# One query buffer per unit with the shift written into it, and one block of values per key step

## The chip, the cores and the metric

The program runs on one core of a Trainium2 chip. The metric is the device time of one execution in microseconds (us), as a median of several runs; smaller is better. The engines are named as the profile names them: PE (TensorE matmuls), PEld (its weight loads), DVE (VectorE), ACT (ScalarE), POOL (GpSimd) and SP (SyncE, which issues DMAs).

## The reference

Two transformer layers on a sequence of S = 2048 rows of D = 128 values. Layer 0: x += attention(norm(x)), causal, 16 heads of 8 values, rotary embedding; then x += a gated network with 512 hidden values and two more 512 x 512 layers. Layer 1: x += attention(norm(x)) over all keys, 16 heads of 8, with low-rank projections and biases; then x += a mixture of 8 experts (top 2). The attention of both layers is, for each head:

```python
scores = einsum('bhsd,bhtd->bhst', q, k) / scale
attn = softmax(scores)          # layer 0: only keys t <= s
out = einsum('bhst,bhtd->bhsd', attn, v)
```

## The kernel before

The program is a row of phases, each a block in which all engines run their own instruction lists, tied by semaphores. The change lies in `attention_phase` (L306), which runs once per layer.

**Units and steps.** The queries are cut into C = 4 column blocks of CW = 512, the heads into G = 4 groups of four. A unit is a column block c with a group g, 16 units per layer in the order of `units`. A unit goes through its keys in steps of 128: 16 steps in layer 1, 4(c + 1) in layer 0, where the last four steps of a unit lie on the diagonal and use only columns from `first_col` on (512, 384, 256, 128 of them). A step has four scores (one per head, j = 0 to 3, below S0 to S3): 64 rows of K against 64 rows of queries, written to a PSUM bank of 512 columns (L442). Heads 0 and 2 lie in rows 0 to 63 of the array, heads 1 and 3 in rows 64 to 127. ACT takes exp of each bank into `probs` (L536), and PE multiplies `probs` with V (`values`, L455), accumulating in the bank `acc`; each head uses 9 columns of its own strip of 32 of the array. A value matmul is float32 and counts as two instructions.

**Precision by split rows.** A block of K or Q holds two heads, each in 64 partitions: products of high and low halves of the numbers in the first 32, and extra rows from `SHIFT_ROW` = 32 on. In these K has ones, and the query buffer the negated maximum of the row (high and low part), so that the score comes out already shifted. There are two query buffers: `Qm` without the shift, used for the maxima, and `Qx` with it, used for the scores.

**Maxima.** For a unit the maximum of each query's scores is wanted before the unit starts. `score_maxima` (L423) makes scores the other way round (queries as weights, 512 keys streaming), two heads into a pair of PSUM banks, and DVE reduces the pair (L556). There are two pairs; the next but one use of a pair waits for its reduction (`m_done`). `plan(n)` spreads the reductions of units n + 1 and n + 2 over the 2 x steps slots of unit n. In layer 1 that is one per slot, in layer 0 it depends on the units' sizes. The last two units have fewer or none. Then DVE forms the negated maxima and writes them to `shiftM` (L576, L580).

**Banks and jobs.** Three PSUM banks (`E_BANKS`) are used in turn by all jobs that ACT evacuates: scores, and query builds. Job e waits until job e - 3 is evacuated:

```python
def wait_bank(e):
    if e >= E_BANKS:
        pe.wait_ge(e_done, e - E_BANKS + 1)
```

PE takes jobs, maxima and values in the order of `unit(n)` (L471): per step, for b = 0 and 1, two scores, then after the first step `build_qm(n + 2)` and after the last but one `build_qx(n + 1)`, then the slot's maxima, then half of the values of the step before (`values_part`, L460; in step 0 of a unit that is the last step of the unit before, and the values of a step 0 and those narrower than 256 columns are one block at b = 1). `build_qm` has for each of two blocks two matmuls (L393, L394), which ACT copies into `Qm` (L515). `build_qx` has the same and four more 128-column matmuls with `shiftM` (L407), and ACT copies into `Qx`. Before the first unit of a layer PE makes the maxima of units 0 and 1 and `build_qx(0)`. In layer 0, POOL masks the diagonal blocks of `probs` (L508) before the values may use them. ACT does the exponentials of step k only when the values of step k - 2 are done (`pv_done`). DVE copies `acc` out once per unit (L584).

## Time and profile before

| | |
|---|---|
| median of 3 runs | 1938.62 us (1923.58 to 1941.95) |
| the profiled execution | 1926.7 us |
| its span, first to last instruction | 1924.8 us |
| mean granted clock of TensorE over the span | 0.892 |
| PE / DVE / ACT / POOL busy | 1793.8 / 1157.7 / 1130.8 / 82.1 us |

Times in the profile are of the one profiled execution, from the first instruction on. A granted clock of 1 is 2.4 GHz, of 0.5 is 1.2 GHz. "PE busy" counts the time in which at least one matmul record is open. A record opens when the matmul's turn has come, so a matmul that waits for its own weight load is counted from then. Matmuls in different halves of the array run side by side, and a merged row of the timeline shows how many (x2, x8) lie in it.

### The profile page before, as it was taken

The numbers are of one execution on the slowest core, as the hardware profiler recorded it, in microseconds if no ns is written. First come the engines' busy times: TensorE is split into PE (matmuls) and PEld (weight loads), VectorE is DVE, ScalarE is ACT, GpSimd is POOL, SyncE is SP. The second block draws the span as 40 slices with busy tenths as digits, with TensorE's granted clock in tenths as the row PEclk, the third lists the DMA queues.
The fourth block names the chain that finished last, engine by engine and source line by source line (L and its number), as shares of the span: only waits on it lengthen the run. The fifth ranks groups of instructions, "written<-read, shape, count | busy, mean of one in ns | idle before, by whom it ended". The sixth has DMA issues, their size and how long they took to land. (4 is left out here: it accounts for less than half of the span.)

```text
span 1924.8 us, 31645 instructions
## 1 busy us (share of the span) xinstructions
PE 1793.8 (93%) x13000; PEld 830.1 (43%) x13000; DVE 1157.7 (60%) x1566; ACT 1130.8 (59%) x2092; POOL 82.1 (4%) x158
## 2 busy tenths in 40 slices
PE   6999999999998999677999999999999999689999
PEld 3544434444334444332333333333333333457676
DVE  7556686777614100469788988988898860611111
ACT  3436566667774322230788878878887887233433
POOL 3011101000000000020000000000000000000000
PEclk9558898888888999775899999999999999789999
DMA  2100000000000000100000000000000000010000
GB/s 98 61 1 2 1 1 1 1 1 1 1 1 1 1 0 0 51 1 0 1 1 1 2 1 1 1 2 1 1 2 1 1 1 1 1 34 11 22 22 22
DMA packets 16766, 17.12 MB, mean 9 GB/s; under 512 B 2994, under 2 KB 13695, under 8 KB 16127
## 3 DMA queue, kind: packets, MB, share of 16 engines
q1 hardware_dynamic: 16639, 15.32, 2.5%
q8 instruction: 93, 1.52, 0.3%
q14 instruction: 34, 0.28, 0.0%
HBM read 14.26 MB, written 1.05 MB: 8 GB/s over the span
## 5 line engine op out<-in xcount | busy, mean ns | idle before, releaser
L556 DVE TENSOR_REDUCE maxp<-banks 128x2 f32<-128x1024 f32 (+3 forms) x800 | 942.7, 1200 | 253.2 <-PE banks L423 145.0
L536 ACT ACTIVATE probs<-banks 128x512 f32<-128x512 f32 (+3 forms) x1664 | 855.7, 571 | 274.8 <-PE banks L442 255.8
L455 PE MATMUL banks<-probs,V 128*9 128x256 f32 (+3 forms) x6272 | 516.0, 403 | 6.9 <-POOL probs L508 6.2
L442 PE MATMUL banks<-Qx,K 64*128 64x512 f32 (+3 forms) x1664 | 460.6, 512 | 6.6 <-ACT probs L536 6.3
L423 PE MATMUL banks<-K,Qm 64*128 64x512 f32 (+3 forms) x1664 | 389.5, 452 | 30.7 <-DVE maxp L556 30.0
L442 PEld LDWEIGHTS banks<-Qx,K 64*128 64x128 f32 x1664 | 188.9, 197 | 390.8 <-ACT probs L536 316.6
L423 PEld LDWEIGHTS banks<-K,Qm 64*128 64x128 f32 x1664 | 187.6, 211 | 83.3 <-DVE maxp L556 67.6
L455 PEld LDWEIGHTS banks<-probs,V 128*9 128x9 f32 x6272 | 93.7, 89 | 261.7 <-ACT probs L536 192.3
L945 DVE SCALAR_TENSOR_TENSOR x<-banks,wts,x 128x128 f32<-128x128 f32 x128 | 36.0, 344 | 195.9 <-PE banks L908 195.9
L933 ACT ACTIVATE work<-banks,eb 128x512 f32<-128x512 f32 x128 | 86.4, 688 | 104.3 <-PE banks L899 101.9
L908 PEld LDWEIGHTS banks<-work 128*128 128x128 f32 x1024 | 118.1, 192 | 11.5 <-issue 11.5
L899 PE MATMUL banks<-xnT,work 128*128 128x512 f32 x256 | 116.0, 601 | 5.0 <-DMA eb<-in_eb 5.0
L908 PE MATMUL banks<-work 128*128 128x128 f32 x1024 | 118.2, 275 | 0.0
L733 PE MATMUL banks<-work,flex 128*128 128x512 f32 x256 | 110.5, 592 | 0.0
L515 ACT ACTIVATE Qx<-banks 128x512 fp32r<-128x512 f32 x64 | 38.2, 597 | 103.6 <-PE banks L407 103.6
L584 DVE COPY outT<-banks 128x512 f32<-128x512 f32 x32 | 21.9, 683 | 97.2 <-PE banks L455 97.2
L771 DVE TENSOR_TENSOR work<-banks,s_rows 128x128 f32<-128x128 f32 x16 | 3.5, 284 | 122.4 <-PE banks L740 122.4
L733 PEld LDWEIGHTS banks<-work,flex 128*128 128x128 f32 x256 | 48.6, 190 | 61.2 <-issue 61.2
L393 PE MATMUL banks<-qb,sel 32*128 32x512 f32 x128 | 69.0, 551 | 6.2 <-PEq L145 3.3
L508 POOL TENSOR_SCALAR_AFFINE_SELECT probs<-probs 128x256 f32<-128x256 f32 x128 | 52.3, 408 | 503.4 <-ACT probs L536 502.8
L899 PEld LDWEIGHTS banks<-xnT,work 128*128 128x128 f32 x256 | 47.6, 194 | 56.3 <-issue 53.1
L756 ACT ACTIVATE work<-banks,sh 128x512 f32<-128x512 f32 x32 | 22.0, 687 | 82.7 <-PE banks L733 82.7
(126 smaller groups left out, 921.6 us busy)
## 6 DMA issues: line engine op xcount, KB each, us to landing
tables<-in_tables SPq DMA_DIRECT2D x2, 2048.0 KB, 9.6
work<-in_ew SPq DMA_DIRECT2D x16, 256.0 KB, 2.9
flex<-in_h SPq DMA_DIRECT2D x2, 1024.0 KB, 7.8
x<-in_x SPq DMA_DIRECT2D x4, 256.0 KB, 4.1
out<-x SPq DMA_DIRECT2D x4, 256.0 KB, 2.3
cst<-in_consts SPq DMA_DIRECT2D x1, 864.5 KB, 5.8
flex<-in_w SPq DMA_DIRECT2D x3, 256.0 KB, 3.0
flex<-in_w_qk SPq DMA_DIRECT2D x1, 256.0 KB, 5.9
```

The lines of the kernel that those rows point to most:

```text
L393: pe.matmul(ebank(e), k.sel[rows, SEL_QHI, b, :], k.qb[rows, 0, c * CW:(c + 1) * CW], start=True, stop=False)
L423: mm = pe.matmul(out, k.Qm[rows, n % 2, b, t * P:(t + 1) * P], k.K[rows, 2 * g + b, a * CW:a * CW + w], start=True, stop=True)
L442: mm = pe.matmul(ebank(e)[:, first:CW], k.K[rows, 2 * g + b, kt * P:(kt + 1) * P], k.Qx[rows, n % 2, b, first:CW], start=True, stop=True)
L455: mm = pe.matmul(acc[32 * j:32 * j + HD + 1, low:high], k.V9[:, kt, g * HG + j, :], k.probs[:, slot + j, low:high], start=(kt == 0), stop= ...
L508: pool.affine_select(out=tile, in_=tile, compare_op=ALU.is_ge, fill=0.0, base=0, pattern=[[0, 2], [1, P]], channel_multiplier=-1).then_inc ...
L515: act.activation(dst, ebank(e), ACT.Copy).then_inc(e_done, 1)
L536: act.activation(k.probs[:, HG * (s % 2) + j, first:CW], ebank(e)[:, first:CW], ACT.Exp, scale=scale).then_inc(e_done, 1)
L556: dve.tensor_reduce(dst, src, AX.X, ALU.max).then_inc(m_done, 1)
L733: mm = pe.matmul(hb[m % 2][:, :], w[:, b, m * P:(m + 1) * P], src[:, b, :], start=(b == 0), stop=(b == HB - 1))
L899: pe.matmul(ub[m][:, :], k.ew1[:, q, m * P:(m + 1) * P], k.xnT[:, c * CW:(c + 1) * CW], start=True, stop=True).then_inc(up_ready, 1)
L908: mm = pe.matmul(yb[c % 2][:, t * P:(t + 1) * P], k.hid[:, c % 2, b, t * P:(t + 1) * P], k.ew2[:, q, b, :], start=(b == 0), stop=(b == HB ...
L933: act.activation(k.hid[:, c % 2, m, :], ub[m][:, :], ACT.Gelu, bias=k.eb1[:, q, m:m + 1]).then_inc(act_ready, 1)
```

## The change

What it does: the two query buffers of a unit become one, `Q`, three deep. `build_queries` writes it without the shift (as `build_qm` did); the maxima read it; later `turn_shift` turns the negated maxima by four 128-column matmuls into one bank, and ACT writes them with two copies (32 partitions, both blocks at once, 2 x 512 columns each) into the rows of `Q` from SHIFT_ROW on. The two blocks of a buffer have shift rows of their own, so the ones of K lie in two rows or the other by the block's parity. In a step, PE now does S0, S1, the first slot's maxima, S2, the second slot's maxima with the upper half of the array first, S3, and then all columns of the values of the step before in one block. In step 0 and in the last but one, S3 comes before the build or the turned shift, and the second slot's maxima after it. The jobs keep their three banks and are numbered from a list.

```diff
@@ -260,7 +260,7 @@
                     low_half(i - 1)
             for r in range(len(rounds)):
                 dve.wait_ge(k_psum, r + 1)
-                dve.tensor_scalar(built(r, 0), k.banks[:, 4 * (r % 2):4 * (r % 2) + 2, :], k.ones_col[:, 0:1], None, ALU.add
+                dve.tensor_scalar(built(r, 0), k.banks[:, 4 * (r % 2):4 * (r % 2) + 2, :], k.ones_col[:, rounds[r][1]:rounds[r][1] + 1], None, ALU.add
                                   ).then_inc(k_built_dve, 1)
 
         @block.gpsimd
...
@@ -326,19 +326,22 @@
     m_base = [sum(len(reductions(m)) for m in range(n)) for n in range(NU + 1)]
     s_base = [sum(steps[:n]) for n in range(NU + 1)]
 
-    e_base = [6]
-    for n in range(NU):
-        e_base.append(e_base[n] + HG * steps[n] + 2 * (n + 2 < NU) + 2 * (n + 1 < NU))
-    qx_after = [steps[n] - 2 for n in range(NU)]
-
-    def qm_job(n, b):
-        return 2 * n + b if n < 2 else e_base[n - 2] + HG + b
-
-    def qx_job(n, b):
-        return 4 + b if n == 0 else e_base[n - 1] + HG * (qx_after[n - 1] + 1) + 2 * (n + 1 < NU) + b
-
-    def exp_job(n, kt, j):
-        return e_base[n] + HG * kt + j + 2 * (kt > 0 and n + 2 < NU) + 2 * (kt > qx_after[n] and n + 1 < NU)
+    shift_after = [steps[n] - 2 for n in range(NU)]
+
+    def exp_bank_jobs():
+        for n in (0, 1):
+            yield from (("queries", n, b) for b in (0, 1))
+        yield ("shift", 0)
+        for n in range(NU):
+            for kt in range(steps[n]):
+                yield from (("scores", n, kt, j) for j in range(HG))
+                if kt == 0 and n + 2 < NU:
+                    yield from (("queries", n + 2, b) for b in (0, 1))
+                if kt == shift_after[n] and n + 1 < NU:
+                    yield ("shift", n + 1)
+
+    e_number = {job: number for number, job in enumerate(exp_bank_jobs())}
+    exp_job = lambda n, kt, j: e_number["scores", n, kt, j]
 
     masks = {n: TC * units[n][0] for n in range(NU)} if causal else {}
     mask_base = lambda n, kt: 2 * (TC * n + kt - masks[n])
...
@@ -386,41 +389,38 @@
                 if e >= E_BANKS:
                     pe.wait_ge(e_done, e - E_BANKS + 1)
 
-            def plain_queries(n, b, e):
+            def build_queries(n):
                 c, g = units[n]
                 rows = slice(32 * g, 32 * g + 32)
+                for b in (0, 1):
+                    e = e_number["queries", n, b]
+                    wait_bank(e)
+                    pe.matmul(ebank(e), k.sel[rows, SEL_QHI, b, :], k.qb[rows, 0, c * CW:(c + 1) * CW],
+                              start=True, stop=False)
+                    pe.matmul(ebank(e), k.sel[rows, SEL_QLO, b, :], k.qb[rows, 1, c * CW:(c + 1) * CW],
+                              start=False, stop=True).then_inc(e_ready, 1)
+
+            def turn_shift(n):
+                e = e_number["shift", n]
                 wait_bank(e)
-                pe.matmul(ebank(e), k.sel[rows, SEL_QHI, b, :], k.qb[rows, 0, c * CW:(c + 1) * CW], start=True, stop=False)
-                return pe.matmul(ebank(e), k.sel[rows, SEL_QLO, b, :], k.qb[rows, 1, c * CW:(c + 1) * CW],
-                                 start=False, stop=True)
-
-            def build_qm(n):
-                for b in (0, 1):
-                    plain_queries(n, b, qm_job(n, b)).then_inc(e_ready, 1)
-
-            def build_qx(n):
                 pe.wait_ge(shift_ready, n + 1)
-                for b in (0, 1):
-                    e = qx_job(n, b)
-                    plain_queries(n, b, e)
-                    for t in range(TC):
-                        mm = pe.matmul(ebank(e)[:, t * P:(t + 1) * P], k.shiftM[:, b, t, :], k.identr[:, :],
-                                       start=False, stop=True, skip_group_check=True)
-                    mm.then_inc(e_ready, 1)
-
-            def score_maxima(n, i):
+                for t in range(TC):
+                    mm = pe.matmul(ebank(e)[:, t * P:(t + 1) * P], k.shiftM[:, t, :], k.identr[:, :], start=True, stop=True)
+                mm.then_inc(e_ready, 1)
+
+            def score_maxima(n, i, halves=(0, 1)):
                 c, g = units[n]
                 t, blocks, a, w, diagonal = reductions(n)[i]
                 m = m_base[n] + i
                 if i == 0:
-                    pe.wait_ge(e_done, qm_job(n, 1) + 1)
+                    pe.wait_ge(e_done, e_number["queries", n, 1] + 1)
                 if m >= 2:
                     pe.wait_ge(m_done, m - 1)
                 for q, b in enumerate(blocks):
-                    for half in (0, 1):
+                    for half in halves:
                         rows = slice(HALF * half, HALF * half + HALF)
                         out = mpair(m)[:, half, q * w:(q + 1) * w]
-                        mm = pe.matmul(out, k.Qm[rows, n % 2, b, t * P:(t + 1) * P],
+                        mm = pe.matmul(out, k.Q[rows, n % 3, b, t * P:(t + 1) * P],
                                        k.K[rows, 2 * g + b, a * CW:a * CW + w], start=True, stop=True)
                     if diagonal:
                         for hh in (0, 1):
...
@@ -437,10 +437,10 @@
                 rows = slice(HALF * half, HALF * half + HALF)
                 e, first = exp_job(n, kt, j), first_col(n, kt)
                 wait_bank(e)
-                if kt == 0 and j in (0, 2):
-                    pe.wait_ge(e_done, qx_job(n, b) + 1)
+                if kt == 0 and j == 0:
+                    pe.wait_ge(e_done, e_number["shift", n] + 1)
                 mm = pe.matmul(ebank(e)[:, first:CW], k.K[rows, 2 * g + b, kt * P:(kt + 1) * P],
-                               k.Qx[rows, n % 2, b, first:CW], start=True, stop=True)
+                               k.Q[rows, n % 3, b, first:CW], start=True, stop=True)
                 mm.then_inc(e_ready, 1)
 
             def values(n, kt, low, high):
...
@@ -457,43 +457,37 @@
                 if high == CW:
                     mm.then_inc(pv_done, 1)
 
-            def values_part(n, kt, b):
-                first = first_col(n, kt)
-                middle = (first + CW) // 2
-                if kt == 0 or CW - first < 2 * P:
-                    if b == 1:
-                        values(n, kt, first, CW)
-                elif b == 0:
-                    values(n, kt, first, middle)
-                else:
-                    values(n, kt, middle, CW)
-
             def unit(n):
                 slots = plan(n)
                 for kt in range(steps[n]):
-                    for b in (0, 1):
-                        scores(n, kt, 2 * b)
-                        scores(n, kt, 2 * b + 1)
-                        if b == 1 and kt == 0 and n + 2 < NU:
-                            build_qm(n + 2)
-                        if b == 1 and kt == qx_after[n] and n + 1 < NU:
-                            build_qx(n + 1)
-                        for m, i in slots[2 * kt + b]:
-                            score_maxima(m, i)
-                        if kt:
-                            values_part(n, kt - 1, b)
-                        elif n:
-                            values_part(n - 1, steps[n - 1] - 1, b)
-
-            build_qm(0)
-            build_qm(1)
+                    scores(n, kt, 0)
+                    scores(n, kt, 1)
+                    for m, i in slots[2 * kt]:
+                        score_maxima(m, i, (0, 1))
+                    scores(n, kt, 2)
+                    if kt == 0 and n + 2 < NU:
+                        scores(n, kt, 3)
+                        build_queries(n + 2)
+                    elif kt == shift_after[n] and n + 1 < NU:
+                        scores(n, kt, 3)
+                        turn_shift(n + 1)
+                    for m, i in slots[2 * kt + 1]:
+                        score_maxima(m, i, (1, 0))
+                    if not (kt == 0 and n + 2 < NU or kt == shift_after[n] and n + 1 < NU):
+                        scores(n, kt, 3)
+                    if kt:
+                        values(n, kt - 1, first_col(n, kt - 1), CW)
+                    elif n:
+                        values(n - 1, steps[n - 1] - 1, first_col(n - 1, steps[n - 1] - 1), CW)
+
+            build_queries(0)
+            build_queries(1)
             for item in first_reductions(0) + last_reductions(0) + first_reductions(1):
                 score_maxima(*item)
-            build_qx(0)
+            turn_shift(0)
             for n in range(NU):
                 unit(n)
-            for b in (0, 1):
-                values_part(NU - 1, steps[NU - 1] - 1, b)
+            values(NU - 1, steps[NU - 1] - 1, first_col(NU - 1, steps[NU - 1] - 1), CW)
 
         if causal:
             @block.gpsimd
...
@@ -510,21 +504,24 @@
 
         @block.scalar
         def _(act):
-            def take_queries(dst, e):
+            def take_queries(n):
+                for b in (0, 1):
+                    e = e_number["queries", n, b]
+                    act.wait_ge(e_ready, e + 1)
+                    act.activation(k.Q[:, n % 3, b, :], ebank(e), ACT.Copy).then_inc(e_done, 1)
+
+            def take_shift(n):
+                e = e_number["shift", n]
                 act.wait_ge(e_ready, e + 1)
-                act.activation(dst, ebank(e), ACT.Copy).then_inc(e_done, 1)
-
-            def take_qm(n):
-                for b in (0, 1):
-                    take_queries(k.Qm[:, n % 2, b, :], qm_job(n, b))
-
-            def take_qx(n):
-                for b in (0, 1):
-                    take_queries(k.Qx[:, n % 2, b, :], qx_job(n, b))
-
-            take_qm(0)
-            take_qm(1)
-            take_qx(0)
+                for half in (0, 1):
+                    rows = slice(HALF * half + SHIFT_ROW, HALF * half + HALF)
+                    copy = act.activation(k.Q[rows, n % 3, :, :],
+                                          ebank(e)[rows, :].unsqueeze(1).to_broadcast([HALF - SHIFT_ROW, 2, CW]), ACT.Copy)
+                copy.then_inc(e_done, 1)
+
+            take_queries(0)
+            take_queries(1)
+            take_shift(0)
             for n in range(NU):
                 for kt in range(steps[n]):
                     s, first = s_base[n] + kt, first_col(n, kt)
...
@@ -536,9 +533,9 @@
                         act.activation(k.probs[:, HG * (s % 2) + j, first:CW], ebank(e)[:, first:CW], ACT.Exp, scale=scale
                                        ).then_inc(e_done, 1)
                     if kt == 0 and n + 2 < NU:
-                        take_qm(n + 2)
-                    if kt == qx_after[n] and n + 1 < NU:
-                        take_qx(n + 1)
+                        take_queries(n + 2)
+                    if kt == shift_after[n] and n + 1 < NU:
+                        take_shift(n + 1)
 
         @block.vector
         def _(dve):
...
@@ -566,13 +563,16 @@
                                       k.maxp[:, n % 2, 0:keys, :, :].rearrange("p a t j -> p (t j) a"), AX.X, ALU.max,
                                       negate=True).then_inc(neg_ready, 1)
 
-            rows_of = lambda part: k.shiftM[:, :, :, :].rearrange("p b t (i s) -> p t b i s", i=2)[:, :, :, :, SHIFT_ROW + part]
+            def rows_of(part):
+                rows = k.shiftM[:, :, :].rearrange("p t (i s) -> p t i s", i=2)[:, :, :, SHIFT_ROW:SHIFT_ROW + 4]
+                return rows.rearrange("p t i (b r) -> p t b i r", b=2)[:, :, :, :, part]
+
             by_block = lambda n: k.negm[:, n % 2, :, :].rearrange("p t (b i) -> p t b i", b=2)
 
             def shift_high(n):
                 dve.wait_ge(neg_ready, n + 1)
                 if n:
-                    dve.wait_ge(e_ready, qx_job(n - 1, 1) + 1)
+                    dve.wait_ge(e_ready, e_number["shift", n - 1] + 1)
                 dve.tensor_copy(rows_of(0), by_block(n)).then_inc(hi_ready, 1)
 
             def shift_low(n):
...
@@ -970,18 +970,18 @@
-        k.Qm, k.Qx = sb("Qm", [P, 2, 2, CW], F32R), sb("Qx", [P, 2, 2, CW], F32R)
+        k.Q = sb("Q", [P, 3, 2, CW], F32R)
-        k.shiftM = sb("shiftM", [P, 2, TC, P], F32R)
+        k.shiftM = sb("shiftM", [P, TC, P], F32R)
-        k.ident64, k.ones_col = sb("ident64", [P, HALF], BF16), sb("ones_col", [P, 1])
+        k.ident64, k.ones_col = sb("ident64", [P, HALF], BF16), sb("ones_col", [P, 2])
```

## Rows read from the trace of the kernel before

**Rows 1.** The page, busy time of each engine (us, share of span, instructions).
```profile
PE 1793.8 (93%) x13000; PEld 830.1 (43%) x13000; DVE 1157.7 (60%) x1566; ACT 1130.8 (59%) x2092; POOL 82.1 (4%) x158
```
**Rows 2.** Busy time by stage: both attentions (us, engines' busy, PEclk, DMA share, GB/s).
```profile
63.00:596.00 533.00, 509.96 (x4278) 220.84 (x4276) 331.41 (x343) 339.93 (x701) 52.27 (x128) 0.82 0.00 1
...
907.00:1632.00 725.00, 715.92 (x6182) 264.21 (x6180) 582.45 (x532) 586.38 (x1085) 0.00 (x0) 0.96 0.00 1
```
**Rows 3.** Timeline of an ordinary step: start us, length us, engine, line, what.
```profile
1206.65 0.50 PE L442 MATMUL banks<-Qx,K 64*128 64x512 f32 x2
...
1206.99 0.40 PE L423 MATMUL banks<-K,Qm 64*128 64x512 f32 x2
1207.25 2.24 ACT L536 ACTIVATE probs<-banks 128x512 f32<-128x512 f32 x4 [0.21 <-PE banks L442]
...
1207.32 0.62 PE L455 MATMUL banks<-probs,V 128*9 128x256 f32 x8
...
1207.87 0.53 PE L442 MATMUL banks<-Qx,K 64*128 64x512 f32 x2
...
1208.56 0.62 PE L455 MATMUL banks<-probs,V 128*9 128x256 f32 x8
1209.11 0.50 PE L442 MATMUL banks<-Qx,K 64*128 64x512 f32 x2
```
**Rows 4.** Timeline of a step of the last unit, without maxima.
```profile
1612.89 0.50 PE L442 MATMUL banks<-Qx,K 64*128 64x512 f32 x2
...
1613.49 2.07 ACT L536 ACTIVATE probs<-banks 128x512 f32<-128x512 f32 x4 [0.16 <-PE banks L442]
...
1613.93 0.70 PE L442 MATMUL banks<-Qx,K 64*128 64x512 f32 x2
...
1614.57 0.62 PE L455 MATMUL banks<-probs,V 128*9 128x256 f32 x8
...
1615.12 0.50 PE L442 MATMUL banks<-Qx,K 64*128 64x512 f32 x2
```
**Rows 5.** Timeline of PE in step 14 of a unit of layer 1, with build_qx.
```profile
1223.83 0.50 PE L442 MATMUL banks<-Qx,K 64*128 64x512 f32 x2
...
1226.28 0.66 PE L407 MATMUL banks<-identr,shiftM 128*128 128x128 f32 x4
1226.87 0.49 PE L393 MATMUL banks<-qb,sel 32*128 32x512 f32 x1
...
1228.12 0.51 PE L423 MATMUL banks<-K,Qm 64*128 64x512 f32 x2
1228.55 0.62 PE L455 MATMUL banks<-probs,V 128*9 128x256 f32 x8
1229.10 0.50 PE L442 MATMUL banks<-Qx,K 64*128 64x512 f32 x2
```
**Rows 6.** Timeline of PE in the same unit: steps 0 and 1, start of 2.
```profile
1187.50 0.50 PE L442 MATMUL banks<-Qx,K 64*128 64x512 f32 x2
...
1191.53 0.50 PE L442 MATMUL banks<-Qx,K 64*128 64x512 f32 x2
...
1193.43 1.05 PE L455 MATMUL banks<-probs,V 128*9 128x512 f32 x8
1194.40 0.50 PE L442 MATMUL banks<-Qx,K 64*128 64x512 f32 x2
```
**Rows 7.** Reductions: group (busy us, mean ns, idle before); timeline of ten in a row.
```profile
L556 DVE TENSOR_REDUCE maxp<-banks 128x2 f32<-128x1024 f32 x736 | 882.9, 1221 | 173.0 <-PE banks L423 145.0 <-PE banks L430 26.3
...
875.18 11.39 DVE L556 TENSOR_REDUCE maxp<-banks 128x2 f32<-128x1024 f32 x10
```
**Rows 8.** Groups by line and shape: the widest ACT copy.
```profile
L302 ACT ACTIVATE K<-banks,ones_col 128x1024 fp32r<-128x1024 f32 x16 | 17.6, 1111 | 5.4 <-PE banks L216 4.9
```
**Rows 9.** Timeline of PE in the 256-column step of a unit of layer 0.
```profile
505.41 0.38 PE L442 MATMUL banks<-Qx,K 64*128 64x256 f32 x2
...
509.80 0.51 PE L455 MATMUL banks<-probs,V 128*9 128x192 f32 x8
510.24 0.33 PE L442 MATMUL banks<-Qx,K 64*128 64x128 f32 x2
```

12 lines of the change are left out of this document (6 added, 6 removed).

## The prediction

> **What bounds the kernel now.** I read the page first: PE is busy 93% of the span, DVE 60%, ACT 59% [rows 1]. Cut by stage, the first attention (63 to 596 us) has PE 96% busy at a mean clock of 0.82, the second (907 to 1632 us) 99% at 0.96 [rows 2]. The two together are 1258 us, and all that the change touches lies in them. Busy is not streaming, though. So next I read the timeline of one ordinary key step of the second attention, PE and ACT together [rows 3]. The reader should see a step as two halves, each a pair of scores (S, L442), a pair of maxima (M, L423) and eight value instructions (V, L455). From S to S it takes 1.22 and 1.24 us, 2.46 together. In another unit the twelve steps from 1194.40 [rows 6] to 1223.83 [rows 5] have a mean of 2.45.
>
> The last unit has no maxima left, and its timeline is the one that decides this case [rows 4]. A half without M would cost PE about 0.43 (S to V) and 0.55 (V to S), 0.98 us. But a step is 2.23 us and not 1.96. The second pair of scores starts at 1613.93, its record is 0.70 long instead of 0.50, and its V comes 0.64 after it and not 0.43. The wait is in `wait_bank`: three score banks rotate, so score S3 takes the bank of S0 and must wait until the exponential of S0 has been done. ACT starts that 0.60 us after S0 (1612.89 to 1613.49), and V follows 1.08 us later: one exponential of 0.60, S3's weight load 0.1, its stream 0.23 and the end of it 0.1, which leaves 0.05 for the hand-over. From S0 to the V behind S3 is therefore **1.68 us**, whatever else PE does. With maxima the same path is in [rows 3]: 1206.65 to 1208.56 is 1.91, that is 1.68 and the 0.23 of the maxima that follow S3. PE hides the latency with V's first half and the first maxima. It is at its bound and at the latency's at once.
>
> DVE is the third candidate: ten reductions back to back take 11.39 us, of which the last counts with its 1.22, so (11.39 - 1.22) / 9 = 1.13 us each [rows 7], 2.26 us per step with two of them. It has 0.2 us to spare.
>
> **The values as one block: every full step gets longer.** The new order is S0, S1, M, S2, half of M, the other half of M, S3, then V over all columns. S3's bank is still S0's, since three banks and the order of their jobs stay. PE now has only S, M, S2 and M to do while it waits. From [rows 3], S to M is 0.34 us and each further pair of matmuls in the halves of the array 0.23 (M to V 0.33 less 0.10 for the end of the stream), so S3's turn comes at 0.34 + 0.23 + 0.23 = 0.80 us. It is let go at 1.68 - 0.43 = 1.25 us, so PE stands 0.45 us. V starts at 1.68. A V of 512 columns to the next S is 0.97 us (1193.43 to 1194.40) [rows 6]. A step costs 1.68 + 0.97 = **2.65 us** where it cost 2.45, or 2.23 without maxima. Said the other way: half of V (0.43) moves out of the wait's cover, and 0.23 of M moves into it.
>
> What the block saves is two changes between the scores' and the values' way of using the array, about 0.1 us each, and one exposed weight load of 0.1. On PE's own account the step is 0.80 + 0.33 + 0.97 = 2.10 us, 0.35 less than now; but these 0.35 are saved ahead of a wait that does not move. The Trainium skill (TensorEngine Tiling, Key Properties) says that a change of tiling mode drains the engine, which the 0.10 here agrees with; by that rule alone 250 steps would give back some 85 us. The same skill (TensorE: Matmul & The Clock Gate, Part 3) says that matmuls start and end in program order, only weight loads being pulled ahead. This speaks against the change, as V could not slip into the wait, and [rows 4] agree: V follows S3 there although its own inputs are older.
>
> Second attention, 16 units of 16 steps: steps 2 to 13 of 14 units, 168 x 0.20 = +33.6 us. Unit 14 has 20 reductions in 32 halves, so between 2.23 and 2.45 now, I take 2.4: 13 x 0.25 = +3. Unit 15: 14 x 0.43 = +6. In step 1, V was one block already (2.87 us, [rows 6]: 1191.53 to 1194.40): 14 x -0.22 = -3. In step 0 the two query builds follow S3 as before, and half of V loses its cover: 4.03 [rows 6] becomes 4.46, 14 x 0.43 = +6.
>
> First attention: a unit of column block c has 4c - 1 ordinary steps, 84 in all. 22 are in the last two units, one without maxima and one with 8 reductions: 11 x 0.43 + 11 x 0.33 = +8. Of the other 62 I take eight to run at the half clock, where PE's own streams take twice the time and cover ACT's latency, which does not grow with them: 0 there. The rest +0.20: +11. Step 1: -2. In the three narrow steps of the diagonal exponentials are shorter and V too: 0, between -0.3 and +0.3 us for each of 48.
>
> **One query buffer: the second build goes.** In step 14 PE builds the shifted queries: twice two matmuls of queries and four turned shifts, 1223.83 to 1229.10 = 5.27 us [rows 5]. After, one block of four turned shifts is left, 0.59 us (1226.28 to 1226.87). Its bank is S1's, whose exponential ends at 0.60 + 0.49 + 0.60 = 1.69, so it starts at 1.74, not 1.68. Then M to V 0.43 and V 0.97: 1.74 + 0.59 + 0.43 + 0.97 = 3.73 us, **-1.54**.
>
> But ACT must now write the shift under both query blocks by two copies of 1024 columns. The trace has such a width at 1111 ns on 128 partitions [rows 8]; on 32 partitions I know no row, so 0.6 (the copy of 512) to 1.11 each, and I take 1.11, the row of the same width. ACT ends the step's fourth exponential near 2.67 us and the copies near 4.7. The next step's S0 starts at 3.73 and would have its exponential at 4.33; it gets it near 4.6, and S2 waits for the copy's bank. Step 15 becomes 2.9 instead of 2.45: +0.42 (0 with the short copies). For 15 builds: 15 x (-1.54 + 0.42) = -17 us.
>
> In the first attention the build is in a step of 256 columns: 4.83 us from 505.41 to 510.24 [rows 9]. After: about 1.25 to the shift (between 0.9, PE's own work, and the 1.68 of full width), 0.59, 0.42 from M to V, and V, whose half of the columns takes 0.44 to the next S (509.80 to 510.24), so 0.76: 3.0, -1.83. The copies hold the 128-column step by 0.35. 15 x -1.48 = -22, and -2 more for those at the half clock.
>
> Before the first unit of each layer the whole build is on the path; it loses a query part but gets the long copies: -1 each, -2.
>
> Other edits are at nothing: the zeroed matrix is half as large, which POOL does under the first loads; the ones column is another column of the same constants; DVE writes the same 16 values; the third query buffer delays nobody, as builds come two units ahead.
>
> **Sum.** Second attention: +33.6 + 3 + 6 - 3 + 6 - 17 = +29. First: 8 + 11 - 2 - 24 = -7. Prologues -2. Together **+20 us**. The profiled execution (1926.7 us, span 1924.8) would become 1947. It lies 12 us under the median of 1938.6, so in medians it is 1959. I name 1952, between them.
>
> **The clock** is the term without a row. A mean of 0.96 over 725 us is 58 us at the half clock, 0.82 over 533 us is 192 [rows 2]. In the second attention part of that follows query builds. A build gets shorter, but PE waits more in every step. All falls of the second attention gone behind the prologue would be some -15 us; one more short fall per unit, at 2 to 3 us for each, +35. I take 0.
>
> **Rivals.** *The wait is not there* (faster): if S0's exponential came in time for 0.80 us, PE would need 2.10, and DVE bounds. It has 2.26 at best. Since the pair of M banks before V is filled late and the next only behind a whole V, a second bound lies at 2.41: M's second half to the next M's result is 0.23 + 0.33 + 0.97 + 0.34 + 0.45 (M's record and the hand-over), then a reduction of 1.13, then 1.38 until a bank is refilled (a reduction's 1.22, hand-over and load), 4.83 for two steps. Against 2.45 that is -0.04 to -0.19 on 222 steps, -9 to -42, with the builds -41: 1926.7 - 67 is about 1860 to 1880. For it speaks how busy PE is; against it [rows 4], where the wait decides with even less work on PE. Chance 0.17.
>
> *The clock stays up* (no change): the wait is as I say, but fewer builds mean fewer falls, -20 over both layers: 1927 by the profiled run. Chance 0.15.
>
> *The clock falls more* (slower yet): PE streams less per time: in a step without maxima two pairs of scores and four passes of half a V, about 0.21 each, 1.3 us of 2.65 and no longer of 2.23. If the clock falls in these 45 steps or once more in each unit, +35: 1982. It decides from one added fall per unit. Chance 0.13.
>
> **Chances.** My forecast has 0.55, from 1935 to 1980. A change within 1% of the time before (19 us) is about what a measurement of this kernel cannot tell from none. My forecast sits on that bound, so a good third of it counts as no change, with nearly all of the second rival: 0.33. Slower by over 1%: the rest and the last rival, 0.48. Faster: the first rival and a little of the second, 0.19. The range of 8 in 10 goes from 1905, which leaves most of the first rival out, to 1988.
>
> **What will show it.** Right: steps of 2.65 us in the second attention with or without maxima; S3 starting 1.25 us after S0, PE's loads waiting on ACT's exponentials (L442's wait longer than now); V 1.68 us after S0; DVE below 85% busy there; the shift step at 3.7. Wrong: steps of 2.1 to 2.45, or reductions back to back, would say that the wait was covered. Copies of 0.6 us would take 6 us off; a mean clock other than 0.96 and 0.82 would move the sum by the clock alone.

## Result: 1.5% slower, by a step of 2.65 us, and the profile after

Over four runs each, the changed kernel has a median of 1962.1 us (1954.9 to 1968.8) and the kernel before 1934.5 us (1923.6 to 1942.0). The ratio is 1.0147, with a 95% interval of 1.008 to 1.0214. The forecast had named 1952 us, within 1935 to 1980. The profiled executions are 1954.9 and 1926.7 us, +28 where the forecast said +20.

The page of the changed kernel, busy time of each engine, in a span of 1953.0 us. It answers to [rows 1].

```profile
PE 1767.4 (90%) x9800; PEld 817.1 (42%) x9800; DVE 1148.0 (59%) x1566; ACT 1127.0 (58%) x2092; POOL 81.5 (4%) x158
```

PE has 3200 instructions less and 26 us less busy time, in a span that is 28 us longer. Every other engine is where it was. So work was taken off PE, and the time did not follow it.

Busy time by stage in the changed kernel, in the columns of [rows 2], with one stretch more: the last unit of the first attention.

```profile
63.00:596.00 533.00, 484.02 (x3134) 200.19 (x3130) 331.05 (x346) 346.15 (x701) 51.98 (x128) 0.83 0.00 1
907.00:1632.00 725.00, 691.07 (x4015) 264.04 (x4015) 577.33 (x535) 556.47 (x1047) 0.00 (x0) 0.96 0.00 1
538.00:590.00 52.00, 47.55 (x156) 11.62 (x156) 0.63 (x1) 26.66 (x52) 1.50 (x4) 0.50 0.00 0
```

PE was busy for 99% of the second attention and is now busy for 95% of it, at the same mean clock. DVE has 80% there (577.33 of 725), so it bounds nothing. The last line is a surprise: 52 us at a granted clock of 0.50. Before, that unit had its first steps at half the clock too, but then came back, and its end ran at 0.91; the same view of the kernel before:

```profile
560.00:590.00 30.00, 29.44 (x248) 9.41 (x240) 0.00 (x0) 24.66 (x49) 1.22 (x3) 0.91 0.01 1
```

From the starts of the scores' first and last instruction (L442) the difference of 28.2 us in the spans divides like this:

| stretch | before | after | difference | forecast |
|---|---|---|---|---|
| up to the first score of the first attention | 69.8 | 70.2 | +0.4 | -1 |
| first attention | 523.6 | 524.6 | +1.0 | -7 |
| between the two attentions | 320.3 | 321.8 | +1.5 | -1 |
| second attention | 716.0 | 739.2 | +23.2 | +29 |
| from its last score to the end | 295.1 | 297.2 | +2.1 | 0 |

Now one ordinary step of the second attention, all engines' timeline in the changed kernel (start us, length us, engine, line, what, and in brackets the idle time before and who ended it). It answers to [rows 3].

```profile
1232.55 0.50 PE L442 MATMUL banks<-Q,K 64*128 64x512 f32 x2
...
1233.13 0.62 PE L423 MATMUL banks<-K,Q 64*128 64x512 f32 x2
1233.15 2.06 ACT L533 ACTIVATE probs<-banks 128x512 f32<-128x512 f32 x4 [0.57 <-PE banks L442]
...
1233.80 0.18 PEld L442 LDWEIGHTS banks<-Q,K 64*128 64x128 f32 x1 [0.48 <-ACT probs L533]
1233.80 0.49 PE L442 MATMUL banks<-Q,K 64*128 64x512 f32 x1
...
1234.22 1.04 PE L455 MATMUL banks<-probs,V 128*9 128x512 f32 x8
...
1235.19 0.50 PE L442 MATMUL banks<-Q,K 64*128 64x512 f32 x2
```

S0 starts at 1232.55 and its exponential at 1233.15. S3 could have come behind the last maxima, near 1233.36 (0.80 us after S0 by the forecast's count), but its weight load stands 0.48 us and is released by ACT's exponential. S3 starts at 1233.80, 1.25 us after S0; V at 1234.22, 1.67 after S0; the next S0 at 1235.19, 2.64 after the last. ACT's four exponentials end at 1235.21, when the next step has just begun, and ACT then has nothing to do until that step's S0 is there. Before this step too it was idle for 0.57 us, where in [rows 3] it was 0.21.

The chief waits over the whole span: first the changed kernel's two (engine, line, who released; us in total, times, longest), then the same two of the kernel before.

```profile
PEld banks L442 <- ACT probs L533: 469.9, 683, 1.7
ACT probs L533 <- PE banks L442: 335.8, 425, 4.4
```
```profile
PEld banks L442 <- ACT probs L536: 316.6, 683, 1.7
ACT probs L536 <- PE banks L442: 255.8, 480, 4.4
```

The scores' weight loads wait on exponentials as often as before, and 153 us longer. ACT waits 80 us longer for scores. Two engines that wait for each other is what a rotation of too few buffers looks like.

### The profile page after: what moved, and what is told of

Same layout as the page of the kernel before. It is cut to its first block and busy times, and to the rows that moved or that the text cites. A ratio compares the mean times of both kernels' runs of the same rounds, so it can differ in the third digit from the quotient of the medians.

```text
span 1953.0 us, 25213 instructions
## 1 busy us (share of the span) xinstructions
PE 1767.4 (90%) x9800; PEld 817.1 (42%) x9800; DVE 1148.0 (59%) x1566; ACT 1127.0 (58%) x2092; POOL 81.5 (4%) x158
## 5 line engine op out<-in xcount | busy, mean ns | idle before, releaser
L553 DVE TENSOR_REDUCE maxp<-banks 128x2 f32<-128x1024 f32 (+3 forms) x800 | 929.7, 1198 | 254.1 <-PE banks L423 163.2
L533 ACT ACTIVATE probs<-banks 128x512 f32<-128x512 f32 (+3 forms) x1664 | 826.4, 577 | 337.6 <-PE banks L442 335.8
L442 PE MATMUL banks<-Q,K 64*128 64x512 f32 (+3 forms) x1664 | 579.7, 488 | 60.4 <-ACT probs L533 32.4
L442 PEld LDWEIGHTS banks<-Q,K 64*128 64x128 f32 x1664 | 240.2, 197 | 596.3 <-ACT probs L533 469.9
L455 PE MATMUL banks<-probs,V 128*9 128x512 f32 (+3 forms) x3328 | 449.0, 614 | 0.0
L423 PE MATMUL banks<-K,Q 64*128 64x512 f32 (+3 forms) x1664 | 393.4, 456 | 39.6 <-DVE maxp L553 39.0
L423 PEld LDWEIGHTS banks<-K,Q 64*128 64x128 f32 x1664 | 188.3, 204 | 106.5 <-DVE maxp L553 83.7
L933 ACT ACTIVATE work<-banks,eb 128x512 f32<-128x512 f32 x128 | 86.3, 687 | 104.5 <-PE banks L899 102.1
L518 ACT ACTIVATE Q<-banks 32x1024 fp32r<-32x1024 f32 x64 | 65.0, 1016 | 69.1 <-PE banks L408 68.4
L455 PEld LDWEIGHTS banks<-probs,V 128*9 128x9 f32 x3328 | 49.8, 89 | 105.3 <-issue 52.2
L132 PE MATMUL banks<-ident,xn 128*128 128x128 f32 x64 | 17.6, 464 | 25.9 <-DVE xn L114 25.9
```

Source lines behind the costliest of these rows:

```text
L423: mm = pe.matmul(out, k.Q[rows, n % 3, b, t * P:(t + 1) * P], k.K[rows, 2 * g + b, a * CW:a * CW + w], start=True, stop=True)
L442: mm = pe.matmul(ebank(e)[:, first:CW], k.K[rows, 2 * g + b, kt * P:(kt + 1) * P], k.Q[rows, n % 3, b, first:CW], start=True, stop=True)
L455: mm = pe.matmul(acc[32 * j:32 * j + HD + 1, low:high], k.V9[:, kt, g * HG + j, :], k.probs[:, slot + j, low:high], start=(kt == 0), stop= ...
L518: copy = act.activation(k.Q[rows, n % 3, :, :], ebank(e)[rows, :].unsqueeze(1).to_broadcast([HALF - SHIFT_ROW, 2, CW]), ACT.Copy)
L533: act.activation(k.probs[:, HG * (s % 2) + j, first:CW], ebank(e)[:, first:CW], ACT.Exp, scale=scale).then_inc(e_done, 1)
L553: dve.tensor_reduce(dst, src, AX.X, ALU.max).then_inc(m_done, 1)
```

## Experiments

### The shift written in place, the step in its old order

The changed kernel, but each half step is two scores, then the build of queries or the turned shift in the second half, then the maxima, then half of the values:

```diff
...
+                    for b in (0, 1):
+                        scores(n, kt, 2 * b)
+                        scores(n, kt, 2 * b + 1)
+                        if b == 1 and kt == 0 and n + 2 < NU:
+                            build_queries(n + 2)
+                        if b == 1 and kt == shift_after[n] and n + 1 < NU:
+                            turn_shift(n + 1)
+                        for m, i in slots[2 * kt + b]:
+                            score_maxima(m, i)
+                        if kt:
+                            values_part(n, kt - 1, b)
...
```

> One query buffer and the shift written in place, but a step in the old order (S0 S1, maxima, half of the values, S2 S3, maxima, the other half). Theory W (the new order is what costs, because S3 waits for the exponential of S0 with all of the values behind it): ordinary steps back at 2.45 us in the second attention, the step with the turned shift near 5.27 - 2.47 + 0.59 = 3.4, the one after it near 3.05 (ACT's two copies), so about 1.3 us saved per build in each layer; time near 1885 (1870 to 1905), 0.975 to 0.985 of the kernel before. Rival C (the shift written in place is what costs, by ACT's copies of 1.0 us each): no better than the kernel before, ratio 1.00 or above.

Measured: a median of 1878.9 us over four runs (1863.7 to 1884.2) beside 1933.0 before, a ratio of 0.9692 (0.9633 to 0.975). So the buffer half of the change is worth a gain of 3.1%, more than the 1.5 to 2.5% expected, and the order of the step turned it into a loss. Ordinary steps are back at 2.45 us. PE and then ACT in steps 14 and 15 of this kernel:

```profile
1198.03 0.52 PE L442 MATMUL banks<-Q,K 64*128 64x512 f32 x2
1198.55 0.66 PE L408 MATMUL banks<-identr,shiftM 128*128 128x128 f32 x4
...
1200.12 0.50 PE L442 MATMUL banks<-Q,K 64*128 64x512 f32 x2
...
1201.77 1.12 PE L442 MATMUL banks<-Q,K 64*128 64x512 f32 x2 [0.36 <-ACT Q L524]
```
```profile
1199.67 2.04 ACT L524 ACTIVATE Q<-banks 32x1024 fp32r<-32x1024 f32 x2
1201.74 1.57 ACT L539 ACTIVATE probs<-banks 128x512 f32<-128x512 f32 x3
```

Step 14 (from 1196.82 to 1200.12) falls from 5.27 [rows 5] to 3.30, but ACT holds its exponentials back for 2.07 us while it copies the shift (1199.67 to 1201.74), and the second half of step 15 waits for the bank: that step (to 1203.60) is 3.48, where 3.05 was expected. The mean clock of the second attention is 0.99 here, where both the kernel before and the changed one have 0.96.

### The new order of the step, two query buffers

The kernel before with nothing but the new order of scores, maxima and values:

```diff
-                    for b in (0, 1):
-                        scores(n, kt, 2 * b)
-                        scores(n, kt, 2 * b + 1)
...
+                    scores(n, kt, 0)
+                    scores(n, kt, 1)
+                    for m, i in slots[2 * kt]:
+                        score_maxima(m, i, (0, 1))
+                    scores(n, kt, 2)
...
+                    for m, i in slots[2 * kt + 1]:
+                        score_maxima(m, i, (1, 0))
...
+                        scores(n, kt, 3)
+                    if kt:
+                        values(n, kt - 1, first_col(n, kt - 1), CW)
...
```

> Two query buffers and the second build as before, but the step in the new order (values as one block behind S3). Theory W: every ordinary step 2.65 us, the step with the second build near 1.68 + 2.47 + 0.43 + 0.97 = 5.55; time 1926.7 + 68 = 1995, up to 2020 if the last unit of the first attention runs at the half clock again; ratio 1.035 to 1.05. Rival C: the order alone is a gain (fewer changes between the two ways of using the array) or at most nothing, ratio at or under 1.00.

Measured: a median of 2040.5 us over five runs (2036.3 to 2063.3), a ratio of 1.0544 (1.0505 to 1.0583). Ordinary steps are 2.64 to 2.65 us. The order alone costs 5.4% on the old buffers, and 4.7% on the new ones (1.0147 / 0.9692). The new order therefore carries the whole loss. The loss is a little above the 3.5 to 5% expected, and more than the steps' lengths at the full clock is in it. In the profiled execution (the slowest of the five, a span of 2061.4 us) the mean clock is 0.857, and the whole last unit of the second attention ran at half. PE in two of its steps:

```profile
1751.82 1.22 PE L442 MATMUL banks<-Qx,K 64*128 64x512 f32 x3
...
1755.90 1.22 PE L442 MATMUL banks<-Qx,K 64*128 64x512 f32 x3
```

4.08 us from step to step, and 1.22 where three scores at the full clock take 0.73 (below). 15 steps of 1.44 us more are 22 us. Its step 14 is 5.70 us at the full clock, and between 6.3 and 7.6 in most units, in which the clock falls.

### Three score banks or five

To give the scores more banks, maxima must give some up. Here are two kernels with one difference between them. Both leave out three quarters of the maxima of the second attention:

```diff
-        out = [(t, (b,), a, CW, False) for a in range(c if causal else C) for t in range(TC) for b in (0, 1)]
+        out = [(t, (b,), a, CW, False) for a in range(c if causal else 1) for t in range(TC) for b in (0, 1)]
...
+        E_BANKS = 3 if causal else 3
+        PAIRS = 2 if causal else 1
...
-        mpair = lambda m: k.banks[:, 3 + 2 * (m % 2):5 + 2 * (m % 2), :]
+        mpair = lambda m: k.banks[:, 3 + 2 * (m % 2):5 + 2 * (m % 2), :] if causal else k.banks[:, 5:7, :]
...
```
```diff
-        E_BANKS = 3 if causal else 3
+        E_BANKS = 3 if causal else 5
```

> The changed kernel, where the second attention takes its maxima over the first 512 keys alone (8 reductions per unit instead of 32, through one pair of banks), so the shift of the softmax is not the true maximum. Three score banks as before. Theory W: the ordinary step stays at 2.65 us although three quarters of PE's maxima and of DVE's reductions are gone. Rival P (the step is PE's own work, its streams and the ends of the streams, or DVE's reductions): steps without maxima 0.46 us shorter, near 2.2.

> The same with five banks in turn for the scores in the second attention, so that S3 takes a bank free since long; nothing else differs. Theory W: the wait is gone, the step falls from 2.65 to ACT's bound of four exponentials, 4 x 0.49 and 0.06, near 2.0 to 2.1 us (PE's own work without maxima 0.34 + 0.33 + 0.97 = 1.64), some 130 us less over the second attention than with three banks. Rival P: no difference between three and five banks.

Measured, one run each: 1953.3 us with three banks and 1744.1 us with five, 209 us apart by one number in the code, and more than the 130 expected. From the first score to the last one the second attentions are 762.8 and 559.8 us long, 203 apart. The first attentions, where the two kernels are the same, differ by 7.5 us. The ordinary steps' lengths (2.64 and 1.96 us below, over 256 steps) make 174 of the 203. What is left goes with the mean clock of the stage, 0.92 and 0.97, and with the steps of the builds. The kernel with three banks is the telling one. Its second attention, busy time as in [rows 2]:

```profile
900.00:1640.00 740.00, 636.10 (x3340) 198.94 (x3332) 158.09 (x176) 558.52 (x1053) 0.00 (x0) 0.92 0.00 1
```

DVE went from 577 to 158 us, PE lost three quarters of the maxima, and the time did not fall: an ordinary step is as long as before, and the stage is 24 us longer than in the changed kernel (762.8 and 739.2), at a lower mean clock. PE in one of its steps:

```profile
1200.13 0.73 PE L444 MATMUL banks<-Q,K 64*128 64x512 f32 x3
1201.38 0.49 PE L444 MATMUL banks<-Q,K 64*128 64x512 f32 x1 [0.51 <-ACT probs L535]
1201.80 1.05 PE L457 MATMUL banks<-probs,V 128*9 128x512 f32 x8
1202.78 0.50 PE L444 MATMUL banks<-Q,K 64*128 64x512 f32 x2
```

S3 starts 1.25 us after S0, V 1.67 after it, the next step 2.65 after it: to 0.01 us the numbers of the step with maxima. It is the bank, and neither PE's work nor DVE's. With five banks, PE in one step and the busy time of the second attention:

```profile
1217.30 0.99 PE L444 MATMUL banks<-Q,K 64*128 64x512 f32 x4
1218.28 1.04 PE L457 MATMUL banks<-probs,V 128*9 128x512 f32 x8
1219.26 0.51 PE L444 MATMUL banks<-Q,K 64*128 64x512 f32 x2
```
```profile
900.00:1430.00 530.00, 517.61 (x3238) 179.89 (x3234) 154.53 (x174) 519.73 (x1024) 0.00 (x0) 0.97 0.00 1
```

The four scores stream as one block (0.99) and a step takes 1.96 us, as much as four exponentials of 0.49. ACT is busy 98% of the stretch. That is the block order's own limit once its wait is covered, in a kernel whose maxima leave the banks free. The real one has no such banks to give: its maxima hold four and `acc` one.

### The old order in the last unit alone

The changed kernel, with the old order (as in the first experiment) in each layer's last unit, the one without maxima:

```diff
-            for n in range(NU):
+            for n in range(NU - 1):
                 unit(n)
+            old_unit(NU - 1)
```

> The changed kernel with only the last unit of each layer in the old order of the step (values in two halves); all other units as changed. In the changed kernel's profile these two units have no maxima, and in the first attention 14 steps of that unit take 4.09 us at the half clock. Theory W with the clock (the wait leaves PE too little to stream, and without maxima the clock does not come back): both units go to 2.22 us a step, 13 x (4.09 - 2.22) + 14 x (2.64 - 2.22) = 24 + 6 = 30 us less, near 1932, ratio to the kernel before 0.995 to 1.005. If the half clock there is chance and not the order's doing: about 12 us less by the full-clock steps alone, or the 4.09 us steps stay, near 1950.

Measured: a median of 1922.3 us over ten runs (1909.5 to 1930.4) beside 1935.1 before, a ratio of 0.9942 (0.9905 to 0.998), just under the 0.995 to 1.005 expected. Against 1.0147 these two units of 32 gave back 2% of the time, some 40 us. PE in the last unit of the first attention, and the busy time of that unit:

```profile
565.29 0.52 PE L442 MATMUL banks<-Q,K 64*128 64x512 f32 x2
...
567.51 0.53 PE L442 MATMUL banks<-Q,K 64*128 64x512 f32 x2
```
```profile
548.00:586.00 38.00, 36.07 (x290) 12.24 (x286) 0.69 (x1) 30.52 (x61) 2.57 (x7) 0.87 0.00 1
```

2.22 us a step, as in [rows 4], and a mean clock of 0.87 over the unit instead of 0.50. The lengths account for 14 x 0.42 us in the second attention and 11 x 0.42 in the first, 10.5 us, and the half clock in the first for some 19 (worked out below). The other 10 us are within what the runs spread. The profiled execution alone, the slowest of the ten, gained only 24.5 us (spans of 1928.5 and 1953.0). Its last unit of the first attention is 38.6 us long instead of 59.6, but the units ahead of it took 13 us more than in the changed kernel, at a mean clock of 0.85 instead of 0.88.

All nine profiles together say more about the half clock than this pair. In the four kernels whose last units have the old order, each of the eight last units was at the full clock from its fifth step on at the latest, and took 34.9 to 38.6 us. With the new order on three banks there are nine last units, in five kernels. Five of them ran at half from their first or second step to their end, and one for 13 of its 16 steps (59.5 to 62.8 us). Two came back after three to seven steps (44.1 and 46.4), and one never fell (38.9). So the order does not decide whether the clock falls there, but it goes with how long it stays down.

### The second copy of the shift on DVE

The first experiment, in which ACT writes the shift under the lower half of the rows and DVE under the upper half:

```diff
-                for half in (0, 1):
+                for half in (0,):
...
+            def copy_upper(n):
+                e = e_number["shift", n]
+                rows = slice(HALF + SHIFT_ROW, 2 * HALF)
+                dve.wait_ge(e_ready, e + 1)
+                dve.tensor_copy(k.Q[rows, n % 3, :, :], ebank(e)[rows, :].unsqueeze(1).to_broadcast([HALF - SHIFT_ROW, 2, CW])
+                                ).then_inc(upper_done, 1)
```

> One query buffer in the old order, with the two copies of the shift rows shared: ACT writes the lower half's, DVE the upper half's, beside each other. In the run with the old order the step after the turned shift took 3.48 us where an ordinary one takes 2.45. Theory A (the first exponential of that step waits for ACT's second copy): it falls to 2.5 to 2.6, 15 times 0.9 us in the second attention and some 15 times 0.4 in the first, 20 us less than with both copies on ACT: near 1860, ratio to the kernel before 0.957 to 0.965. Rival D (DVE, which has 0.2 us per step to spare, becomes late with its reductions instead): the 1.0 us comes back in the reductions of the next steps, ratio 0.969 or above.

Measured: a median of 1817.7 us over four runs (1815.0 to 1825.2), a ratio of 0.9437 (0.9375 to 0.95). This is the fastest of all with the whole computation in it: 5.6% under the kernel before and, by the two ratios (0.9437 / 1.0147), 7.0% under the changed one. It is also well under the 1860 us expected. All engines' timeline of steps 14 and 15:

```profile
1140.54 1.23 DVE L600 CAST Q<-banks 32x1024 fp32r<-32x1024 f32 x1 [0.43 <-PE banks L411]
...
1140.96 1.01 ACT L528 ACTIVATE Q<-banks 32x1024 fp32r<-32x1024 f32 x1
...
1141.41 0.51 PE L446 MATMUL banks<-Q,K 64*128 64x512 f32 x2
...
1142.00 2.23 ACT L543 ACTIVATE probs<-banks 128x512 f32<-128x512 f32 x4
...
1144.06 0.50 PE L446 MATMUL banks<-Q,K 64*128 64x512 f32 x2
```

The two copies lie side by side, and the next step's S0 (1141.41) has its exponential 0.59 us later (1142.00): it is held up no more. Step 14 is 3.30, step 15 2.65 (1141.41 to 1144.06) instead of 3.48. 15 x 0.83 is 12 us, and the second attention is 13 us shorter than in the first experiment. The first attention is 47.7 us shorter, far more than its steps can explain (the 128-column step lost 0.97 us, 15 x 0.97 = 15). A part may be the spread of the runs, as the first experiment's profiled execution (1884.1 us) is at the slow end of its four (from 1863.7). The rest goes with the clock. The first attention in this kernel, then in the first experiment:

```profile
63.00:530.00 467.00, 437.95 (x4150) 184.41 (x4148) 350.01 (x359) 334.40 (x685) 52.02 (x128) 0.92 0.01 1
```
```profile
63.00:530.00 467.00, 437.39 (x3761) 187.83 (x3760) 329.63 (x338) 316.15 (x621) 45.49 (x112) 0.81 0.00 1
```

PE is busy equally long in both, but at a mean clock of 0.92 instead of 0.81, and it gets 10% more instructions done. That a shorter wait behind each build is what keeps the clock up is the nearest reading; no run separates it from chance or from the rest.

### The same copy on DVE, in the changed kernel

> The changed kernel, values still as one block behind S3, with the shift copies shared between ACT and DVE. Theory A: the step after the turned shift falls from 3.07 to 2.65 us in the second attention and by about 0.6 in the first, 15 us together, and up to 35 more by the clock in the first attention, as in the old order, where sharing them gave 61 us of which the steps' lengths at full clock explain 20. So 1915 to 1947, ratio 0.99 to 1.005, and with it the new order still costs 5% or more against the same kernel in the old order (1818). Theory W': if the wait for S0's exponential was made worse by ACT's copies, other steps than that one would get shorter too; W says that the 2.65 us steps stay.

Measured: four runs between 1913.1 and 1956.2 us, median 1937.9, beside a median of 1937.5 before (1923.9 to 1953.9 in seven runs); they spread too much for an interval to be given, so no more is read from the total than that it lies near the kernel before, as expected. Against the same kernel in the old order (1817.7) even the mean of the two shorter runs (1913.1 and 1925.9) is 5.6% more. All engines' timeline of its step 15:

```profile
1193.17 3.49 DVE L557 TENSOR_REDUCE maxp<-banks 128x2 f32<-128x1024 f32 x3
...
1193.20 0.50 PE L446 MATMUL banks<-Q,K 64*128 64x512 f32 x2
...
1194.45 0.50 PE L426 MATMUL banks<-K,Q 64*128 64x512 f32 x2 [0.28 <-DVE maxp L557]
...
1196.08 0.50 PE L446 MATMUL banks<-Q,K 64*128 64x512 f32 x2
```

Step 15 is 2.88 us where the changed kernel has 3.07; it is not the 2.65 expected, because DVE is late with its reductions after the copy and the second block of maxima must wait for it before S3 can be issued. Ordinary steps stay at 2.64: whatever is done about the build, the block order keeps its wait. In the profiled execution the first attention is 37 us shorter than in the changed kernel (487.6 and 524.6), 21 of them in its last unit, which this time did not fall to the half clock. The second is 13 us longer, because there the last unit ran at half throughout (62.8 us where it was 44.1).

## Why the prediction was right, step by step

**The wait behind `wait_bank` decides: shown.** The prediction read 1.68 us from S0 to the V behind S3 out of a step in which nothing else was left to do [rows 4], and added V's 0.97 [rows 6]. The changed kernel has 1.67 and 0.97. That it is the bank and not PE or DVE was shown by taking the maxima out (2.65 stays) and by adding banks (1.96). With this the first rival, in which PE would need 2.10 and DVE 2.41, is out. That rival had PE's busy share on its side, and the share was of no use: PE was 99% busy before and the step still had no room, since its work was also the cover of ACT's latency.

**The shift step: right.** Forecast 3.73 us for step 14 with 1.74 us to the turned shift; PE in the changed kernel:

```profile
1235.19 0.50 PE L442 MATMUL banks<-Q,K 64*128 64x512 f32 x2
...
1236.92 0.66 PE L408 MATMUL banks<-identr,shiftM 128*128 128x128 f32 x4
...
1238.92 0.50 PE L442 MATMUL banks<-Q,K 64*128 64x512 f32 x2
...
1242.00 0.50 PE L442 MATMUL banks<-Q,K 64*128 64x512 f32 x2
```

1.73 to the shift and 3.73 in all. The step with 256 columns in the first attention is 3.01 us against 3.0 forecast.

**Step 15: right in kind, 0.2 us short.** It is 3.08 here (1238.92 to 1242.00) where 2.9 was forecast; 15 x 0.2 is 3 us. ACT's side of it, in the changed kernel:

```profile
1237.88 2.04 ACT L518 ACTIVATE Q<-banks 32x1024 fp32r<-32x1024 f32 x2
1239.94 2.06 ACT L533 ACTIVATE probs<-banks 128x512 f32<-128x512 f32 x4
```

A copy is 1.02 us, near the 1.11 taken from [rows 8] and far from the short end of 0.6. The two run from 2.69 us after S0 to the next exponential at 4.75. That is 1.02 after the next S0 instead of 0.60, so the hold-up is 0.42, and the step is longer than 2.65 by 0.43: the exponentials pass the whole delay on. The forecast had put S0's exponential near 4.6, 0.15 too early. Its own numbers do not give that: 2.67 and two copies of 1.11 are 4.89, a hold-up of 0.56. By its own terms the step would have been 3.2 us; with copies of 1.02 it is 3.08. The miss of 0.2 us is a slip in the sum, and not in the mechanism.

**Step 0: 4.28 and not 4.46.** The query builds run closer together: from the start of the first to the maxima behind them it is 1.15 us (1290.35 to 1291.50), where the kernel before took 1.31 (1189.23 to 1190.54, in the step of [rows 6]). 14 x 0.18 is 3 us less. Step 1 was right, 2.65.

**Second attention: +23.2 and not +29.** Step 15 (+3) and step 0 (-3) cancel, and the ordinary steps are as forecast. The clock's falls have moved: before, they lay in steps 14 and 15, behind the long build, in eight units of 16 (unit 4: 6.30 and 4.25 us instead of 5.27 and 2.45), and after, in steps 0 and 1, behind the query builds, in six units (unit 1: 5.00 and 3.11 instead of 4.28 and 2.65), and in the change from unit 14 to the last one. Summed over such steps, the falls cost some 17 us before and 14 after. (Both sums hold a wait of PE for DVE's shift in step 14 of unit 14, which is no matter of the clock.) That is 3 of the missing 6; the other 3 are below what the rows can tell.

**First attention: +1.0 and not -7, by a term that was set to nothing.** In the last unit, twelve steps of full width from 537.80 to 587.12 ran at the half clock: 49.3 us where 12 x 2.65 is 31.8, so 17.5 more, and with the narrow steps behind them some 19. The whole unit took 59.6 us and, in the kernel before, 38.6. One such step, PE's timeline in the changed kernel:

```profile
554.42 1.22 PE L442 MATMUL banks<-Q,K 64*128 64x512 f32 x3
...
556.69 1.89 PE L455 MATMUL banks<-probs,V 128*9 128x512 f32 x8
558.51 1.22 PE L442 MATMUL banks<-Q,K 64*128 64x512 f32 x3
```

This is the mechanism of the last rival, the clock that falls in the steps without maxima, and in one of the two last units it stayed down to the end (in the other for three steps). Ahead of it the clock did better than before: its mean is 0.87 from 63 to 538 us, where the kernel before had 0.82 from 63 to 560, and 0.05 x 475 is 24 us of gain. That is a rough estimate, as if everything took twice as long at half the clock; the step above takes 4.09 and not 5.3. So the term that was taken as 0 is +19 and about -24, two large parts that nearly cancel. The other terms then come to about +6 and not to -7 (1.0 - 19 + 24). Of these 13 us two parts can be named. A step of 128 columns takes 2.11 us at the full clock where it took 1.34, so 0.77 more and not 0.35; over 15 of them that is 6 us. With one of ACT's two copies on DVE it takes 1.55, so most of the 0.77 is ACT's copies. And in units 6, 7, 10 and 11 (counted from 0) there are steps with three reductions instead of two, in which PE waits for DVE. One of them in the changed kernel, PE's timeline, from its S0 at 343.69 to the next S0:

```profile
345.75 0.50 PE L423 MATMUL banks<-K,Q 64*128 64x512 f32 x2 [0.85 <-DVE maxp L553]
...
347.38 0.50 PE L442 MATMUL banks<-Q,K 64*128 64x512 f32 x2
```

It takes 3.69 us at the full clock where the same step took 3.32, and in units 10 and 11 nine such steps are 3 us longer in all. The forecast has no such steps. It has eight at the half clock instead, with nothing added; but in the kernel before none of these ordinary steps ran at half from start to end. The stage's total came out near the forecast by parts that cancel, and that was luck. The +19 is the part that the experiment on the last units took away.

**The clock rival in between** (the clock stays up because builds are shorter) was right about the buffers: with the old order, the second attention's mean rose from 0.96 to 0.99, which over 685 us is, as a rough estimate, 0.03 x 685 = 20 us, the size it had in the forecast for both layers. With the new order the mean is 0.96 again. That the half microsecond of waiting in each step is why, is only argued.

**The prologues: 0 and not -2**, too small to follow.

The two halves of the change were priced apart in the forecast, a build that gets shorter and a step that gets longer. Alone they measured -3.1% and +5.4%, together +1.5%. So the mechanism and the size of the step's loss were foreseen; that the sum of the first attention fit was not.

## What to carry to other kernels

Count, for each rotating buffer, the time from its request to its reuse, and the work that the order puts between the two. Here it is 1.25 us over three banks, and half of the values was what covered it; an order that saves PE 0.35 us by joining blocks, but puts them behind the wait instead of inside it, makes the step longer by 0.2. A step in which an engine has little to do, as in the last unit here, shows such a latency bare, and it tells more than a busy share of 99%. When a build is made shorter by giving another engine longer copies, look at what that engine does next: sharing the copy between ACT and DVE turned -3.1% into -5.6%.

## What the runs showed of the chip that was not expected

- The same steps without maxima ran in two ways, 2.64 us at the full clock and 4.09 at half. In the changed kernel the second attention's last unit took the first way after three steps, and the first attention's the second to its end; in the changed kernel with the copy on DVE it was the other way round. A step at the full clock, from the second attention's last unit of the changed kernel, to hold against the 4.09 above:

```profile
1625.50 0.73 PE L442 MATMUL banks<-Q,K 64*128 64x512 f32 x3
...
1628.14 0.73 PE L442 MATMUL banks<-Q,K 64*128 64x512 f32 x3
```

- At half the clock such a step is 1.44 us longer. In the old order it is 3.39 us at half the clock and 2.22 at full, and there the unit came back to the full clock by its fifth step each time, while in the new order it mostly stayed at half.
- ACT's copy of 1024 columns on 32 partitions takes 1.02 us, nearly as much as the 1.11 on 128 in [rows 8]; DVE's takes 1.23. The 0.09 between the two of ACT need not come from the partitions: the instruction of [rows 8] also reads a bias (`ones_col`). In the kernel before, ACT's instructions of 128 x 512 that read a bias take 0.69 us (L933) and those without one 0.60 (L515), the same 0.09 apart.
- The clock's falls follow other work than before: the long builds at a unit's end then, the query builds at its start now, and the stretch without maxima. Fewer instructions in one place did not remove them but moved them.
- Moving one copy of 1 us off ACT, 16 times in the first attention, went with a mean clock of 0.92 there instead of 0.81, and with 47.7 us, three times the copies' own 16. In the new order the same edit went with 0.91 instead of 0.84 there. Each is one profiled execution of one kernel, and the kernels' runs spread by 10 to 43 us.
